# Keys folded into the queries' product, two image buffers, and a TensorE loop of two images a turn

## What is computed

```python
h = _group_norm(x, gn_w, gn_b).reshape(B, C, H * W)
qkv = jnp.einsum('oc,bcn->bon', qkv_w, h) + qkv_b[None, :, None]
q, k, v = jnp.split(qkv, 3, axis=1)
attn = jax.nn.softmax(jnp.einsum('bcn,bcm->bnm', q, k) * scale, axis=-1)
h = jnp.einsum('bcm,bnm->bcn', v, attn)
h = jnp.einsum('oc,bcn->bon', proj_w, h) + proj_b[None, :, None]
x = x + h
```

## Time and profile before

| what | us |
|---|---|
| median of 3 executions | 2303.35 (2302.36 to 2305.99) |
| span of the profiled execution | 2300.8 |
| PE busy | 2104.3 (91%) |
| ACT busy | 1747.7 (76%) |
| DVE busy | 1712.9 (74%) |
| POOL busy | 1272.4 (55%) |

### The profile page before, as it was taken

The page is one execution under the profiler, slowest core; times in us unless marked ns, Lnnn a source line. Parts: engine busy times, 40 slices in busy tenths (PEclk is TensorE's granted clock), DMA queues, the critical chain, the costliest instruction groups (busy, mean ns, idle before and its releaser), DMA issues.

```text
span 2300.8 us, 59519 instructions
## 1 busy us (share of the span) xinstructions
PE 2104.3 (91%) x21394; PEld 1564.6 (68%) x21394; DVE 1712.9 (74%) x5284; ACT 1747.7 (76%) x3393; POOL 1272.4 (55%) x1576
## 2 busy tenths in 40 slices
PE   5899999999999999999999999999999999999984
PEld 3567767667767667767667767667767667767663
DVE  6677777777777777777777777777777777777753
ACT  3688777778777878777778777788777788777763
POOL 5356555556555556555556555556555556555554
PEclk9999999999999999999999999999999999999997
DMA  1111111111111111111111111111111111111110
GB/s 37 37 33 34 42 42 33 46 37 32 42 41 32 46 37 32 41 41 33 46 37 32 42 41 32 46 37 32 41 41 33 46 37 32 41 42 32 46 29 24
DMA packets 76188, 86.84 MB, mean 38 GB/s; under 512 B 20624, under 2 KB 55440, under 8 KB 76048
## 3 DMA queue, kind: packets, MB, share of 16 engines
q1 hardware_dynamic: 76048, 85.48, 14.3%
HBM read 18.29 MB, written 16.78 MB: 15 GB/s over the span
## 4 chain that ended last, share of the span: by engine, by line
PE 72%; DVE 19%; ACT 3%; issue 2%; SPq 2%; DMA 1%; POOL 1%; POOLq 0%; ACTq 0%; DVEq 0%
PE ps L996 17%; PE ps L1092 10%; PE ps L888 9%; PE ps L890 9%; PE ps L889 9%; PE ps L1060 5%; PE ps L952 4%; PE ps L1042 3%; PE ps L1008 2%; DVE cm L728 2%; DVE e L801 2%; DVE smax L799 2%; DVE et L820 2%; DVE ssum L809 2%; DVE xl L778 2%
## 5 line engine op out<-in xcount | busy, mean ns | idle before, releaser
L996 PE MATMUL ps<-vg,p 128*128 128x129 f32 x4096 | 539.9, 279 | 0.0
L996 PEld LDWEIGHTS ps<-vg,p 128*128 128x128 f32 x4096 | 505.6, 192 | 49.5 <-issue 13.7
L407 POOL TENSOR_SCALAR nmean<-mv 128x4 f32<-128x4 f32 x256 | 58.4, 228 | 677.8 <-DVE mv L766 677.7
L728 DVE TENSOR_REDUCE cm<-ps 128x1 f32<-128x512 f32 x512 | 336.6, 680 | 49.5 <-PE ps L952 47.8
L549 ACT ACTIVATE p<-ps 128x512 f32<-128x512 f32 x512 | 297.9, 588 | 42.8 <-PE ps L890 41.4
L542 ACT ACTIVATE ps<-shift 128x512 f32<-128x512 f32 x512 | 301.3, 597 | 20.7 <-ACT p L549 1.1
L409 POOL TENSOR_TENSOR rstd<-veps,halfpow 128x4 f32<-128x4 f32 x256 | 266.0, 1039 | 0.0
L1092 PEld LDWEIGHTS ps<-w,hid 128*128 128x128 f32 x2048 | 234.4, 192 | 30.5 <-ACT hid L601 30.5
L1092 PE MATMUL ps<-w,hid 128*128 128x128 f32 x2048 | 241.5, 276 | 8.6 <-ACT hid L601 8.6
L952 PE MATMUL ps<-kgh,qgh 128*128 128x512 f16 x512 | 181.7, 391 | 64.3 <-DVE qgl L722 62.4
L592 ACT ACTIVATE oh<-ps 128x512 f16<-128x512 f32 x64 | 38.2, 597 | 214.6 <-PE ps L1060 214.6
(11 more groups left out here) (180 smaller groups left out, 5599.5 us busy)
## 6 DMA issues: line engine op xcount, KB each, us to landing
ptbd<-et SPq DMA_DIRECT2D x512, 64.0 KB, 2.0
x_sb<-in_x SPq DMA_DIRECT2D x32, 512.0 KB, 3.8
kbd<-kk SPq DMA_DIRECT2D x512, 32.0 KB, 2.0
out_y<-o_sb SPq DMA_DIRECT2D x64, 256.0 KB, 2.5
e<-in_w_t SPq DMA_DIRECT2D x1, 256.0 KB, 3.8
w<-in_w_t SPq DMA_DIRECT2D x1, 256.0 KB, 3.8
hid<-in_in_w_t SPq DMA_DIRECT2D x1, 192.0 KB, 2.4
hid<-in_qkv_w_t SPq DMA_DIRECT2D x1, 128.0 KB, 3.1
```

What stands on the lines that cost most here:

```text
L728: v_.reduce_max(cm[:, c // 2, c % 2:c % 2 + 1], bank("max", c), X).then_inc(s["max_out"], 1)
L996: last = mm(ps[:, b, at:at + PVW], p32[:, c % PRING, part], vg32[:, j, :], start=j == 0 and q % 2 == 0, stop=j == MT - 1, skip_group_check ...
```

## The change

With the bias of the keys left out (it adds the same to all scores of a query, which the softmax takes away), the scores are `h^T Wq^T Wk h` plus a term from the bias of the queries. So the product of the two weight matrices, `G`, is made once in the prologue, `qg` multiplies `h` by `G`, and `h` itself (`hh`, `hl`) stands in the place of the keys:

- The steps `kg:0` and `kg:1` are gone from PE, ACT and DVE. All other words of `PROGRAM` stand where they stood, with their banks.
- `max` and `st` read `hh` and `hl` in place of `kgh` and `kgl`. Since `st` of one image then still reads them while the next is normalised, `hh`, `hl`, `qgh` and `qgl` have two buffers, chosen by the parity of the image. Their writers wait for `st` and `vg` of the image two before.
- A buffer's number must be known when PE's program is written, so PE's loop now holds two iterations (step 2 in `Fori`, 14 turns for the same 28 iterations).
- The prologue turns two raw weight matrices on PE, copies them, multiplies them, and splits the product in its two parts.

The diff, cut to its core (the renaming of weight slots, of lines and of the names of raw weights is left out):

```diff
@@ PROGRAM, pe
-        score0:0@5- score1:0@3- pv:13- pv:14- pv:15- kg:0@4 kg:1@3 v:0@2- turn_q:1@5-- qg:0@4 vg:0@5 max:0@4
+        score0:0@5- score1:0@3- pv:13- pv:14- pv:15- v:0@2- turn_q:1@5-- qg:0@4 vg:0@5 max:0@4
@@ def iterations(engine, images)
+    if engine == "pe" and (last - first) % 2:
+        first += 1
@@
-        hh, hl = sb("hh", [P, N], F16), sb("hl", [P, N], F16)
-        qgh, qgl = sb("qgh", [P, N], F16), sb("qgl", [P, N], F16)
-        kgh, kgl = sb("kgh", [P, N], F16), sb("kgl", [P, N], F16)
+        hh, hl = sb("hh", [P, 2, N], F16), sb("hl", [P, 2, N], F16)
+        qgh, qgl = sb("qgh", [P, 2, N], F16), sb("qgl", [P, 2, N], F16)
@@ def run
-            def iteration(kind, i):
+            def iteration(kind, i, number):
                 for name, index, off in steps_of(key, None if kind == "steady" else i, images):
                     if name in table:
+                        side[key] = (number + off) % 2
                         table[name](kind, i + off, index)
...
-                with engine.Fori(loop.start, loop.stop) as i:
-                    iteration("steady", i)
+                with engine.Fori(loop.start, loop.stop, 2) as i:
+                    iteration("steady", i, loop.start)
+                    iteration("steady", i + 1, loop.start + 1)
@@ gn2 on POOL; on ACT alike, for hh
-                if due(value := upto(img - 1, 2, per=2)):
+                if due(value := upto(img - 2, 2 * MT, per=2 * MT)):
+                    pool.wait_ge(s["st_mm"], value)
+                if due(value := upto(img - 2, 2, per=2)):
                     pool.wait_ge(s["vg_mm"], value)
-                g.tensor_tensor(hl[:], h32[:], hh[:], ALU.subtract).then_inc(s["h_lo"], 1)
+                g.tensor_tensor(hl[:, img % 2], h32[:], hh[:, img % 2], ALU.subtract).then_inc(s["h_lo"], 1)
@@ prologue on DVE
-                halves(QG)
-                halves(KG)
+                dve.wait_ge(s["setup_mm"], 1)
+                link(v_.tensor_copy(z[:, 0, 0:2 * P], ps[:, 6, 2 * P:4 * P]))
                 gn2(None, 0, 0)
...
+                dve.wait_ge(s["setup_mm"], 2)
+                link(v_.tensor_copy(wh[:, G, :], ps[:, ST_BANKS[0], 0:P]))
+                link(v_.tensor_tensor(wl[:, G, :], ps[:, ST_BANKS[0], 0:P], wh[:, G, :], ALU.subtract))
+                link(v_.tensor_copy(col(QGB), ps[:, ST_BANKS[0], P:P + 1]))
@@ prologue on PE
+                nc.tensor.transpose(ps[:, 6, 2 * P:3 * P], wraw[:, QG, :], identf[:])
+                nc.tensor.transpose(ps[:, 6, 3 * P:4 * P], wraw[:, KG, :], identf[:]).then_inc(s["setup_mm"], 1)
                 gn2(None, 0, 0)
+                pe.wait_ge(s["setup_dve"], 1)
+                mm(ps[:, ST_BANKS[0], 0:P], rows_q, rows_k, start=True, stop=True)
+                mm(ps[:, ST_BANKS[0], P:P + 1], rows_k, col(QGB), start=True, stop=True).then_inc(s["setup_mm"], 1)
@@ row_max on PE
-                if c < 2:
-                    pe.wait_ge(s["kg_hi"], upto(img, c + 1, per=2))
-                mm(bank("max", c), qgh[:, P * (c // 2):P * (c // 2 + 1)], kgh[:, HALF * (c % 2):HALF * (c % 2 + 1)],
+                m = side["pe"]
+                mm(bank("max", c), qgh[:, m, P * (c // 2):P * (c // 2 + 1)], hh[:, m, HALF * (c % 2):HALF * (c % 2 + 1)],
@@ st on PE
-                three(bank("st", c), kgh[:, keys], kgl[:, keys], qgh[:, queries], qgl[:, queries],
+                m = side["pe"]
+                three(bank("st", c), hh[:, m, keys], hl[:, m, keys], qgh[:, m, queries], qgl[:, m, queries],
```

More of the change, by code:

```diff
@@ L62 @@
         ln_q:0-- pv:7- ln_in:0- quant:0-- down:1-- turn_in:0- gn0:0 k:0- ln_q:1-- gn1:0 q:0- gn2:0 quant:1--
-        score0:0- score1:0- prob0:0- pv:15- kg:0 ln_in:1- turn_p0:0- prob1:0- qg:0""",
+        score0:0- score1:0- prob0:0- pv:15- ln_in:1- turn_p0:0- prob1:0- qg:0""",
     "act": """
@@ L68 @@
         turn_in:0- seed:11- norm_out:1-- k:0- st:10- seed:12- st:11- turn_q:0-- seed:13- st:12- seed:14- q:0- st:13-
-        seed:15- quant:1-- gn2:0 st:14- st:15- ffn:0-- score0:0- score1:0- kg:0 kg:1 turn_q:1-- v:0- qg:0 bias_x:0
+        seed:15- quant:1-- gn2:0 st:14- st:15- ffn:0-- score0:0- score1:0- turn_q:1-- v:0- qg:0 bias_x:0
         vg:0 norm_in:1- ffn:1-- turn_in:1- qg:1 k:1- pv1:0- q:1- v:1- shift:0 seed:0 seed:1 vg:1 st:0 turn_x:0
@@ L163, in sem @@
             return ctx.enter_context(nc.semaphore(name))
-        QG, KG, VG, PROJ, Q, K, V, OUT, PVG = range(9)
-        wh, wl = sb("wh", [P, 9, P], F16), sb("wl", [P, 9, P], BF16)
+        QG, KG, VG, PROJ, RQ, RK, RV, ROUT = range(8)
+        G, PVG, Q, K, V, OUT = range(6)
+        wh, wl = sb("wh", [P, 6, P], F16), sb("wl", [P, 6, P], BF16)
         w1h, w1l = sb("w1h", [P, FF], F16), sb("w1l", [P, FF], BF16)
@@ L236, in build @@
         w1raw, kraw = e[:, 0, 0, :], et[:, 0, 0, 0:P]
+        rows_q, rows_k = z[:, 0, 0:P], z[:, 0, P:2 * P]
         ones = res[:, 0, 0, :]
@@ L276, in spread @@
             return ap.unsqueeze(2).to_broadcast([P, 2 * HEADS, WIN])
+        side = {}
         before = tenants(images)
@@ L519, in step @@
                     act.wait_ge(s[name + "_mm"], upto(img, c + 1, per=2))
-                    sc.activation(dst[:, HALF * c:HALF * (c + 1)], bank(name, c), ACT.Identity,
+                    if due(value := upto(img - 2, 2 * MT, per=2 * MT)):
+                        act.wait_ge(s["st_mm"], value)
+                    sc.activation(dst[:, img % 2, HALF * c:HALF * (c + 1)], bank(name, c), ACT.Identity,
                                   bias=col(bias)).then_inc(s[name + "_hi"], 1)
@@ L859, in quant @@
                 v_.tensor_scalar(expo[:, h], expo[:, h], E4M3_MIN_NORMAL, ROUND_3_BITS, ALU.max, ALU.mult).then_inc(s["expo_low"], 1)
-            run(dve, "dve", {"gn0": gn0, "gn1": gn1, "gn2": gn2, "qg": global_lo("qg", qgh, qgl, QGB),
-                      "kg": global_lo("kg", kgh, kgl, KGB), "max": row_max,
+            run(dve, "dve", {"gn0": gn0, "gn1": gn1, "gn2": gn2, "qg": global_lo("qg", qgh, qgl, QGB), "max": row_max,
                       "maxima": maxima, "pv": pv, "ln_in": ln_in,
@@ L924, in step @@
                     part = slice(HALF * c, HALF * (c + 1))
-                    three(bank(name, c), wh[:, w, :], wl[:, w, :], hh[:, part], hl[:, part]).then_inc(s[name + "_mm"], 1)
+                    m = side["pe"]
+                    three(bank(name, c), wh[:, w, :], wl[:, w, :], hh[:, m, part], hl[:, m, part]).then_inc(s[name + "_mm"], 1)
                 return step
@@ L932, in vg @@
                     part = slice(HALF * c + P * j, HALF * c + P * (j + 1))
-                    last = three(bank("vg", c)[:, P * j:P * (j + 1)], hh[:, part], hl[:, part], wh[:, PVG, :], wl[:, PVG, :])
+                    m = side["pe"]
+                    last = three(bank("vg", c)[:, P * j:P * (j + 1)], hh[:, m, part], hl[:, m, part], wh[:, PVG, :], wl[:, PVG, :])
                 last.then_inc(s["vg_mm"], 1)
@@ L974, in st @@
                     pe.wait_ge(s["qg_lo"], upto(img, h + 1, per=2))
-                if h == 0 and j % HT == 0:
-                    pe.wait_ge(s["kg_lo"], upto(img, j // HT + 1, per=2))
                 keys, queries = slice(P * j, P * (j + 1)), slice(HALF * h, HALF * (h + 1))
-                three(bank("st", c), kgh[:, keys], kgl[:, keys], qgh[:, queries], qgl[:, queries],
+                m = side["pe"]
+                three(bank("st", c), hh[:, m, keys], hl[:, m, keys], qgh[:, m, queries], qgl[:, m, queries],
                       first=False, skip_group_check=True).then_inc(s["st_mm"], 1)
```

51 lines of the change are left out of this document (26 added, 25 removed).

## The result

| | before | changed |
|---|---|---|
| time, median (lowest to highest) | 2302.86 us (2300.49 to 2305.99) | 2369.97 us (2368.7 to 2376.23) |
| span of the profiled execution | 2300.8 us | 2368.2 us |
| granted TensorE clock, mean over the span | 0.983 | 0.968 |

The ratio is 1.0298, 95% interval 1.0283 to 1.0312: the change costs 67 us. Slower was forecast, but with 2327 us, and the range ended at 2346.

The account below looks back on a forecast made before the run. PE was taken to bound most of an iteration and DVE a part. From 2303.35 us, 13 branch fetches add 26.0, 18 images gain 9.9, clock and prologue add 7.3: 2327 us; own range 2304 to 2346, 8-in-10 range 2284 to 2346.

Parts of the forecast that it names:

- The sum on record: Whole kernel: 2303.35 + 26.0 for branch fetches - 9.9 for the fold + 7 clock + 0.3 prologue, 2327 us.
- What bounds the kernel, and the code: PE and DVE chain, both kgl on it; PE's doubled loop of 10.9 pieces isn't held, so 13 taken branches fetch.
- What a fetch costs: At PE's branch back: 3.3 us a fetch (1.3 to 3.8), turning y 2.0 us late in 13 images.
- The rival of two fetches in a row: At each PE branch the piece after the loop's head is missing too: 13 x 5.3, 2374 us; chance 0.08.
- DVE's two `kgl`: DVE ahead of max:0 and xl: their removal gains 0.55 us an image, bounds 0.2 and 0.76.
- Matmuls of `kg`: PE's six matmuls, 1.3 us an image, are hidden ahead of max:0's wait; removing them is worth nothing.
- the clock term: PE idles longer ahead of max:0 and at the branch: six more falls to 1.2 GHz, 7 us in all.
- none to twelve: Bounds on the extra clock falls in PE's loop, 0 to 14 us.
- The prologue: Two turnings, a copy and a product ahead of the first qg, four splits gone: 0.3 us later.

Follow-up runs that it names:

- c1: The fold with PE's loop of one image a turn and single buffers, POOL copying hh and hl for st, against before: 2307.7 us, ratio 1.0024.
- u2: The changed kernel with PE's loop written out, so no branch and each code piece fetched once: 2336.2 us, ratio 1.0139 to before.
- h1: The changed kernel with a hint for PE's branch back armed at the head of each turn: 2334.5 us, ratio 1.0135 to before.
- k0: The kernel before with the keys' product left out, kgh and kgl filled once from image 0, output not the reference's: 2306.6 us, ratio 1.0019.
- c2: c1 with eight matmuls that nobody reads put into PE's wait ahead of max:0: 2286.5 us, ratio 0.9930 to before.
- f0: The kernel before with eight matmuls that nobody reads put into PE's wait ahead of max:0: 2295.7 us, ratio 0.9971.
- u3: c3 with PE's loop written out, so no branch and each code piece fetched once: 2309.4 us, ratio 1.0037 to before.
- c3: c1 with qg:0 in PSUM bank 3 instead of 4, so max:0 need not wait for qgl: 2279.9 us, ratio 0.9905 to before.
- b2: The kernel before with only PE's loop doubled to two images a turn, keys' product and single buffers kept: 2383.5 us, ratio 1.0340.

## Why the prediction was wrong

In medians the 67 us are: the fold in a loop of one image, 5 (c1 over before); the fetching, 27 to 29 (u2 and h1 over c1); the stall, 34 to 36 (changed over u2 and h1). The sum on record had 26.0 - 9.9 + 7 + 0.3 = 23.

- **What bounds the kernel, and the code.** Right. Both `kgl` were on the path, the doubled code doesn't stay, and 13 branches stall (3.41 to 4.29 us each). But the images without a branch don't gain in the changed kernel: they take 69.8 us on average against 69.0 before. The gain shows only where the code stays (c1, k0).
- **What a fetch costs.** The branch was priced at 3.3 us of bounds 1.3 and 3.8; 3.8 was measured, the upper bound. With 3.8 the turning is 2.5 us late. Against an iteration that gains 0.55 that makes 13 x 3.05 = 40 us for the stall, and 13 x 2.55 = 33 by the 3.3 that I took; u2 and h1 show 34 to 36. In the trace the turning of `y` starts 4.48 us after `max:0` on average (3.95 to 4.90), where the sum has 4.1 with 3.3 and 4.6 with 3.8. This step was about right in size. Not all of the stall's price is waiting, though. The 13 images with a stalled branch all have half clock at their head, ten for 6.8 us (73.8 us an image) and three for about half as long (73.1); h1's images with a fall take 70.8. So, as an estimate, 13 x 2.3 = 30 us is stall at equal clock, and the rest comes with the longer half clock. The rival of two fetches in a row gave 2374, near the time, but for a wrong reason: in each of the 13 branch rows there is one packet of q8, not two. It starts 0.9 to 1.4 us after the branch and takes 0.9 to 1.7, and the branch ends 1.2 to 1.5 us after it.
- **DVE's two `kgl`.** 0.55 us an image forecast; 0.43 measured where nothing disturbs, and 0.31 on average (c2 against f0), inside the bounds of 0.2 and 0.76. Over-sized by a fifth to two fifths.
- **Matmuls of `kg`: "They stay worth nothing", and the clock term.** This failed in its size. Hidden work on PE had a worth in the clock. The sum had it as a term of 7 us for six more falls. c1 has seven more (12 in place of 5), so their number came out, but their price did not: against undisturbed images they cost 19.7 us in c1 and 7.3 before. That is 12 us more, as much as the fold gains in the images (28 x 0.43), and the sum had taken 9.9 off for the fold. The 1.2 us a fall were 7.2 divided by six, though the sixth, at 2159.88, lies behind the 27 periods; by five they are 1.4, and the eleven in the distances of c1 come to 1.8 each. In the changed kernel the falls are 17, the upper end of "none to twelve" more, and they last 92 us in place of 17. f0 and c2 confirm the worth of keeping PE busy from the other side.
- **The step that is missing.** The sum charged a fetch only where PE stalls. The pieces fetched along the way, 11 a turn by my count and 13 in the trace, stood at nothing, as for PE they come in time. They do, but they meet SP's DMA issues on the way, which carry the keys to `score1:1` and the probabilities to `pv0:1`. That is 27 to 30 us, and it is why the time lies outside the range. With it the sum comes to some 2355; of the 15 us left, by estimate, the fold's smaller gain is 7 (31 x 0.24) and the dearer falls are 5. The rows for it were there: before has 9 issues over 0.7 us, and 7 of them overlap a packet of q8, all before 250 us or after 2166 us, when PE meets code for the first time. 2374 being close to the time is luck for the same reason: that rival has no such term.
- **The Trainium skill.** "Runtime: NRT & Kernel Launch", section Instruction fetch mechanics, was cited for a stall at a taken branch whose target isn't held; the 3.8 us of the branch row agree that there is a stall. They don't agree with the 128 KiB as a measure of what a loop may have: the loop of 7.5 pieces, 120 KB, was fetched anew in each turn. Nor do they with "the current 2-page window" of the section, as the loop of 5.5 pieces branches back in 0.21 us. The same section says of a long kernel that the sequencer streams it and that crossing into the next 16 KiB block is "mostly hidden". u3 against c3 shows where that ends: hidden on PE's own side, but 30 us by way of SP's issues for 144 more pieces.
- **The prologue.** 0.3 us more forecast. The loop's second iteration starts 1 us earlier in c1 than before (branch rows at 296.0 and 297.0). Too small to matter.

A part is still open. u2 and h1 spend 10 to 17 us more at half clock than c1, so some of their 27 to 29 us may be clock, and c1 has other buffers than they; only u3 against c3 is free of both. The changed kernel's stall and clock are parted above by an estimate alone. That a packet of PE's code holds up an issue of SP is shown by the ends, 0.37 us apart. What both of them need, and why 86 meetings pass without it, no run shows.

## To carry over

Before a loop's body is doubled to give buffers constant addresses, compare its code with what is known to stay: here 5.5 pieces of 16 KB stayed and 7.5 did not, and a copy by an idle engine (c1) freed the fold of the doubled loop at no measurable cost (k0, without copies, is no faster). Charge code that is fetched again not only at its branch but at whatever issues DMAs on the path. Before hidden work is taken off TensorE, ask what the wait that remains does to its clock, and whether another bank can split that wait: the fold became worth 22 us with that, and 16 with fillers.

## What the runs showed of the hardware

- A taken branch of PE back to code that has to be fetched takes 3.4 to 4.3 us (median 3.8), with one packet of code in it (up to 5.2 in b2, where six of 13 rows hold two packets); with a hint at the head of the turn, 0.36; where the code stays, 0.21.
- A loop of 5.5 pieces is fetched once; one of 7.5 costs nine pieces a turn, one of 8.5 ten, one of 10.9 thirteen (twelve with the hint).
- Of SP's DMA issues, 0.59 us each, 56 take 0.7 to 2.0 us in the changed kernel. 54 of them overlap a packet of PE's code (0.9 to 1.9 us) and end 0.25 to 0.39 us after it. 86 others overlap one and aren't lengthened.
- Eight matmuls of no use in a wait of PE, 1.7 us an image, made the kernel before 0.3% faster and the folded one 0.9%; one wait of 2.30 us had 12 falls to 1.2 GHz in 28 images, three of 0.28, 0.23 and 1.21 in its place none.
